# Last projection of a four-layer graph network: centring and scaling of four tiles on GpSimd, VectorE's order laid out anew, transposes one product earlier

## The reference

```python
x_attn = x_attn @ W_proj + b_proj
y = x + x_attn
mu = jnp.mean(y, axis=-1, keepdims=True)
var = jnp.mean(jnp.square(y - mu), axis=-1, keepdims=True)
return (y - mu) * jax.lax.rsqrt(var + LN_EPS) * gamma + beta
...
x = x + _L3_gnn_ref(...) + _L3_mix_ref(xn[None], ...)[0]
x = x + _L3_ffn_ref(_layernorm(x, axis=-1)[None], L3_ffn_Wg, L3_ffn_W1, L3_ffn_W2)[0]
```

## Time and profile before

| | |
|---|---|
| median of three runs | 2966.78 us (2961.51 to 2971.74) |
| span of the profiled execution | 2958.9 us |
| median less span | 7.9 us |
| TensorE busy | 2721.0 us, 92% |
| VectorE busy | 1415.1 us, 48% |
| ScalarE busy | 1128.2 us, 38% |
| GpSimd busy | 704.2 us, 24% |
| this stage's first and last product on TensorE | 2734.86, to 2771.97 |
| its last transposes | 2780.71 to 2782.19 |

### The profile page before, as it was taken

How to read it: one execution, slowest core, us unless ns; L and a number is a source line. 1 busy time by engine, 2 the same in 40 slices (tenths; PEclk the granted TensorE clock), 3 DMA queues, 4 the chain that set the end, 5 groups by cost and what they waited for, 6 DMA issues and landing times.

```text
span 2958.9 us, 48747 instructions
## 1 busy us (share of the span) xinstructions
PE 2721.0 (92%) x20003; PEld 2472.4 (84%) x20003; DVE 1415.1 (48%) x3609; ACT 1128.2 (38%) x2106; POOL 704.2 (24%) x260
## 2 busy tenths in 40 slices
PE   8999999997769999998999899989997999999797
PEld 8999999994339878998888899989676888795697
DVE  8777565573122135568733632231665564105632
ACT  6633265551003213329431342232654243445231
POOL 0134311110002412220334143324112341103121
PEclk9999999998799999999999999999999999999899
DMA  2022221017981112220121122212001121100121
GB/s 69 12 76 79 86 71 38 30 46 280 414 333 57 59 33 55 65 83 26 44 69 50 60 65 76 76 54 76 17 9 52 54 81 49 36 22 23 33 65 59
DMA packets 163790, 220.37 MB, mean 74 GB/s; under 512 B 21521, under 2 KB 142795, under 8 KB 163570
## 3 DMA queue, kind: packets, MB, share of 16 engines
q1 hardware_dynamic: 163570, 217.26, 22.1%
HBM read 215.31 MB, written 1.92 MB: 73 GB/s over the span
## 4 chain that ended last, share of the span: by engine, by line
PE 58%; DVE 7%; ACT 3%; DMA 2%; issue 2%; POOL 1%; SPq 0%; DVEq 0%; ACTq 0%; POOLq 0%
PE ps L58 41%; PE ps L1968 3%; DMA expert_regions<-in_L_ffn_w 2%; PE ps L1882 2%; PE ps L2134 1%; PE ps L2272 1%; PE ps L2155 1%; PE ps L690 1%; PE ps L609 1%; PE ps L599 1%; ACT buf L1079 1%; PE ps L698 1%; DVE buf L2011 1%; DVE buf L2020 1%; PE ps L2916 1%
## 5 line engine op out<-in xcount | busy, mean ns | idle before, releaser
L58 PE MATMUL ps<-weights_r,buf_r 128*125 128x256 f32 (+3 forms) x4050 | 538.6, 284 | 5.7 <-POOL weights_r L276 1.9
L276 POOL TENSOR_TENSOR weights_r<-weights,weights_r 128x1536 fp32r<-128x1536 f32 (+1 forms) x79 | 273.6, 3463 | 1042.8 <-ACT weights_r L269 1029.4
L58 PEld LDWEIGHTS ps<-weights_r,buf_r 128*125 128x125 f32 (+1 forms) x4050 | 508.1, 186 | 9.0 <-issue 4.2
L276 POOL TENSOR_TENSOR weights_r<-weights,head_weights_r 128x1536 fp32r<-128x1536 f32 (+1 forms) x77 | 270.3, 3510 | 1021.7 <-ACT head_weights_r L269 1013.2
L58 PE MATMUL ps<-xT_r,weights_r 128*128 128x376 f32 (+1 forms) x2100 | 345.4, 310 | 0.0
L58 PEld LDWEIGHTS ps<-xT_r,weights_r 128*128 128x128 f32 x2100 | 313.4, 188 | 4.8 <-issue 2.8
L58 PE MATMUL ps<-head_weights_r,buf_r 128*125 128x256 f32 (+2 forms) x2310 | 316.1, 283 | 0.0
L58 PEld LDWEIGHTS ps<-head_weights_r,buf_r 128*125 128x125 f32 x2310 | 293.3, 187 | 0.0
L58 PE MATMUL ps<-weights_r,xT_r 128*125 128x256 f32 x1680 | 233.3, 282 | 8.0 <-issue 4.8
L269 ACT ACTIVATE head_weights_r<-weights 128x1536 fp32r<-128x1536 f32 (+1 forms) x77 | 112.8, 1465 | 306.1 <-PE ps L58 193.1
L58 PEld LDWEIGHTS ps<-weights_r,xT_r 128*125 128x125 f32 x1680 | 212.8, 186 | 10.3 <-issue 5.4
(11 more groups left out here) (368 smaller groups left out, 4310.2 us busy)
## 6 DMA issues: line engine op xcount, KB each, us to landing
expert_regions<-in_L_ffn_w SPq DMA_DIRECT2D x64, 576.0 KB, 15.3
expert_regions<-in_L_ffn_w SPq DMA_DIRECT2D x48, 768.0 KB, 20.5
weights<-in_L_mix_fc_w SPq DMA_DIRECT2D x24, 768.0 KB, 4.5
weights<-in_L_gnn_W SPq DMA_DIRECT2D x18, 768.0 KB, 4.6
weights<-in_L_ffn_W SPq DMA_DIRECT2D x12, 768.0 KB, 4.7
weights<-in_L_mix_w_mapT SPq DMA_DIRECT2D x9, 768.0 KB, 4.8
weights<-in_L_gnn_W_out SPq DMA_DIRECT2D x9, 768.0 KB, 4.5
weights<-in_L_mix_kqv_wT SPq DMA_DIRECT2D x9, 768.0 KB, 4.6
```

The lines of the kernel that those rows point to most:

```text
L58: mm = net.nc.tensor.matmul(ps, net.r(stationary(s, k)), net.r(moving(m, k)), start=(n == 0 and k == 0), stop=(stop and n == 2 and k == kc ...
L276: self.nc.gpsimd.tensor_tensor(self.r(load.dst), load.dst, self.r(load.high), ALU.subtract).then_inc(self.low_made, 1)
```

## The change

`scaled` of tiles 0 to 3 leaves VectorE. GpSimd does it in two steps, `centred` (y - mean, a tensor_scalar with the column of means) and `scaled` (times the row of gamma, a tensor_tensor), each 125 x 768, behind `mean`; `sum` waits for the second. Tile 4 keeps its one-instruction `scaled` on VectorE, now ahead of `inverse`. VectorE's other steps are laid out anew: inverse, sum, stats, mean2 of tile t-1 come behind the second moments of tile t; inverse2 and shift of tile t-1 behind the mean of tile t. ScalarE follows: high(t-2) and root2(t-1), then root(t), then norm(t-1), and at the end high(3) comes ahead of root2(4). TensorE's turn(t-2) comes behind product(0, t). GpSimd waits for gamma and does its eight steps between the two places where it splits weights.

```diff
-        self.order = {e: [] for e in ("pe", "act", "dve")}
-        pe, act, dve = (self.order[e] for e in ("pe", "act", "dve"))
+        self.order = {e: [] for e in ("pe", "act", "dve", "pool")}
+        pe, act, dve, pool = (self.order[e] for e in ("pe", "act", "dve", "pool"))
         for t in range(NT):
             for n in range(len(units)):
                 pe.append(("product", NT * n + t))
-                if n == 1 and t > 1:
+                if n == 0 and t > 1:
                     pe += [("turn", t - 2, g) for g in range(2)]
                 dve += [("add", NT * n + t), ("moments", NT * n + t)]
-                if n == 0 and t > 0:
-                    dve += [("inverse2", t - 1), ("shift", t - 1)]
-                    act += [("norm", t - 1)] + [("high", t - 2, g) for g in range(2) if t > 1]
+                if n == 1 and t > 0:
+                    dve += [("inverse", t - 1), ("sum", t - 1), ("stats", t - 1, 0), ("stats", t - 1, 1), ("mean2", t - 1)]
+                    act += [("high", t - 2, g) for g in range(2) if t > 1] + [("root2", t - 1)]
             dve.append(("mean", t))
+            act.append(("root", t))
+            if t < NT - 1:
+                pool += [("centred", t), ("scaled", t)]
+            if t > 0:
+                dve += [("inverse2", t - 1), ("shift", t - 1)]
+                act.append(("norm", t - 1))
             if t > 1:
                 dve += [("low", t - 2, g) for g in range(2)]
-            dve += [("inverse", t), ("scaled", t), ("sum", t), ("stats", t, 0), ("stats", t, 1), ("mean2", t)]
-            act += [("root", t), ("root2", t)]
-        dve += [("low", NT - 2, g) for g in range(2)] + [("inverse2", NT - 1), ("shift", NT - 1)] + [("low", NT - 1, g) for g in range(2)]
-        act += [("high", NT - 2, g) for g in range(2)] + [("norm", NT - 1)] + [("high", NT - 1, g) for g in range(2)]
-        pe += [("turn", t, g) for t in (NT - 2, NT - 1) for g in range(2)]
+        last = NT - 1
+        dve += [("scaled", last), ("inverse", last), ("sum", last), ("stats", last, 0), ("stats", last, 1), ("mean2", last)]
+        dve += [("low", last - 1, g) for g in range(2)] + [("inverse2", last), ("shift", last)] + [("low", last, g) for g in range(2)]
+        act += [("high", last - 1, g) for g in range(2)] + [("root2", last), ("norm", last)] + [("high", last, g) for g in range(2)]
+        pe += [("turn", t, g) for t in (last - 1, last) for g in range(2)]
...
             elif kind == "scaled":
+                dve.wait_ge(done.sem, done.issued)
                 dve.wait_ge(self.gamma.sem, self.gamma.value)
...
             elif kind == "sum":
                 dve.wait_ge(done.sem, done.issued)
+                if t < NT - 1:
+                    dve.wait_ge(self.net.pool.sem, self.at["pool"]["scaled", t])
...
     def gpsimd(self, pool):
         self.net.split_low(self.weights[-1].unit, self.weights[-1].segment)
+        pool.wait_ge(self.gamma.sem, self.gamma.value)
+        nc, done = self.nc, self.net.pool
+        for kind, t in self.order["pool"]:
+            if kind == "centred":
+                self.wait(pool, "dve", "mean", t)
+                ins = nc.gpsimd.tensor_scalar(self.y[:, t], self.y[:, t], self.net.mv[:, t, 0:1], None, ALU.subtract)
+            else:
+                pool.wait_ge(done.sem, done.issued)
+                ins = nc.gpsimd.tensor_tensor(self.y[:, t], self.y[:, t], self.gamma.dst[:TP, 0], ALU.mult)
+            ins.then_inc(done.sem, done.one())
         for load in self.weights[1:]:
             self.net.split_low(load.unit + 2, load.segment)
```

More of the change, by code:

```diff
@@ L1122, in __init__ @@
                 pe.append(("product", NT * n + t))
-                if n == 1 and t > 1:
+                if n == 0 and t > 1:
                     pe += [("turn", t - 2, g) for g in range(2)]
                 dve += [("add", NT * n + t), ("moments", NT * n + t)]
-                if n == 0 and t > 0:
-                    dve += [("inverse2", t - 1), ("shift", t - 1)]
-                    act += [("norm", t - 1)] + [("high", t - 2, g) for g in range(2) if t > 1]
+                if n == 1 and t > 0:
+                    dve += [("inverse", t - 1), ("sum", t - 1), ("stats", t - 1, 0), ("stats", t - 1, 1), ("mean2", t - 1)]
+                    act += [("high", t - 2, g) for g in range(2) if t > 1] + [("root2", t - 1)]
             dve.append(("mean", t))
+            act.append(("root", t))
[4 more added lines that the diff above has]
+                act.append(("norm", t - 1))
             if t > 1:
                 dve += [("low", t - 2, g) for g in range(2)]
-            dve += [("inverse", t), ("scaled", t), ("sum", t), ("stats", t, 0), ("stats", t, 1), ("mean2", t)]
-            act += [("root", t), ("root2", t)]
-        dve += [("low", NT - 2, g) for g in range(2)] + [("inverse2", NT - 1), ("shift", NT - 1)] + [("low", NT - 1, g) for g in range(2)]
-        act += [("high", NT - 2, g) for g in range(2)] + [("norm", NT - 1)] + [("high", NT - 1, g) for g in range(2)]
-        pe += [("turn", t, g) for t in (NT - 2, NT - 1) for g in range(2)]
-        bases = dict(pe=net.pe.planned, act=net.act.planned, dve=net.dve.planned)
+        last = NT - 1
[3 more added lines that the diff above has]
+        pe += [("turn", t, g) for t in (last - 1, last) for g in range(2)]
+        bases = dict(pe=net.pe.planned, act=net.act.planned, dve=net.dve.planned, pool=net.pool.planned)
         self.at = {e: {q: bases[e] + i + 1 for i, q in enumerate(seq)} for e, seq in self.order.items()}
```

## The result

The changed kernel takes 2969.07 us (median of 20 runs, 2965.41 to 2973.63), beside 2964.50 us for the kernel before in as many runs of the same series. The ratio is 1.0017, its 95% interval 1.0010 to 1.0023: some 5 us slower (3 to 7). In a later series, with some of the experiments, the same kernel gave 1.0029 (1.0019 to 1.0038). The forecast was 5.95 us slower, 2972.7 us.

A forecast was written before the change was run, and what follows sets the result against it. TensorE was taken to bound the stage up to the last product, VectorE's chain the tail; mean(4) +6.26 us and tail -0.31 gave +5.95, so 2966.78 + 5.95 = 2972.7 us, range 2964 to 2980.

The forecast's parts named there:

- What bounds: In the stage, TensorE sets the time up to the last product, 6.96 us a tile; a shorter VectorE list buys nothing.
- The loop: Turn, product 1, VectorE's block, third add, mean, shift, norm, next turn: 8.72 us against TensorE's 6.96, so TensorE waits.
- GpSimd's pair: centred 2.13 us, gap 0.26, scaled 1.82; hidden in the loop with 0.96 us to spare, costing 0.30 on tile 0.
- Rival 1: GpSimd late: centred takes 2.94 us, tile 0's sum comes 0.81 later; +6.8 us, 2973.5 us; chance 10%.
- Rival 3: GpSimd's centred, just ahead of VectorE's shift, holds it by the shared port: 2.17 us three times, 2979.2 us; chance 6%.
- The clock in the loop: TensorE about 80% busy in the loop keeps full clock, so nothing charged; 3 us of spread to either side carried.
- The tail: From mean(4) to turn(4), 7.37 us against 7.68 before: net -0.31, as high(3) no longer stands behind root2(4).
- The sum: Waits and tail added up: mean(4) +6.26 us, turn(4) at 2786.66, +5.95, everything behind it unchanged.

The follow-up runs named there:

- e5_both_back: Changed kernel with turn behind product 1 again and scaled back on VectorE, leaving VectorE's and ScalarE's new order; ratio 1.0004 to the kernel before.
- e9_first_on_dve: Changed kernel with scaled of tile 0 alone back on VectorE, behind mean(0), tiles 1 to 3 staying on GpSimd; ratio 1.0016 to the kernel before.
- e3_scaled_on_dve: Changed kernel with scaled of every tile back on VectorE, behind low(t-2), new orders and the turn's earlier place kept; ratio 1.0005 to the kernel before.
- e7_loop_longer: Changed kernel with nothing on GpSimd and scaled on VectorE between inverse and sum, inside the loop; ratio 1.0029 to the kernel before.
- e1_turn_back: Changed kernel with turn(t-2) behind product 1 of tile t again, VectorE's new order and GpSimd's steps kept; ratio 1.0012 to the kernel before.

## Why the prediction was right, point by point

- *What bounds.* Right. TensorE set the time up to the last product: e5_both_back, with VectorE's order changed and its load full, ends as the kernel before. That a shorter VectorE list brings nothing is shown inside the loop only: three scaled on GpSimd or on VectorE give the same places (e9_first_on_dve, e3_scaled_on_dve). In the old order no run took them off VectorE.
- *The loop.* Right in kind, and nearly in size: 8.72 us forecast, 8.84 and 8.80 measured in the two profiles, 8.80 with the clock undisturbed. The third add was to stand 6.08 behind the turn's start and stands 6.26 and 6.21 behind it in the two tiles at full clock (2769.25 - 2762.99, 2778.04 - 2771.83). e7_loop_longer shows that it is this loop: one instruction moved into it and 1.0 us more each time. turn(0) was forecast at 9.50 from mean(0) and came at 9.49.
- *GpSimd's pair.* 2.13 + 0.26 + 1.82 = 4.21 forecast, 2.21 + 0.08 + 1.85 = 4.14 measured, sum(0) at 4.67 behind mean(0) against 4.60. Rival 1 (2.94 for centred) did not occur. That the pair is hidden in the loop, with 0.96 to spare, held: tile 2's ended at 2765.75, 1.26 ahead of its sum (2767.01). What I did not see is that 4.60 and the 3.16 from sum to mean are a loop of their own, 7.7 long, ready to bind as soon as the first is cut; I had both terms on the page and used them for tile 0 only. It cost the forecast nothing and the expectation of e1_turn_back 3 us.
- *The port.* Rival 3 did not occur: shift took 212 to 215 ns in all five tiles, as before. In three of them GpSimd's centred started beside it (2761.57 and 2761.61, 0.17 before shift's end), and took 2.20 us, against 2.21 in tile 0 with no shift beside it: neither held the other. But shift was first each time, by 0.04 us, and rival 3 priced the other order, which these two instructions have in no run. For GpSimd first, the evidence is five of the sixty rows of 125x1, those from 2075.3 to 2079.2: the other fifty-five ran with GpSimd idle. The Trainium skill's sentence that tensor_scalar can take both ports (SBUF — State Buffer, "Who interferes with whom") showed in none of these 125x1 rows; whether it would with centred first stays open.
- *The clock in the loop.* Wrong: "I charge nothing for the loop". It fell once, behind the first wait, and cost 1.49 us (10.33 - 8.84). The row that I leaned on the earlier trace rows is of a stretch whose waits are shorter (1.39 to 1.56 us within it, 1.75 just ahead of it) than the first one here (1.90). A mean share over 10 us didn't carry over to a single longer gap. The spread of 3 us that I carried for the clock, reckoned for the tail, took it in.
- *The tail.* 7.37 forecast, 7.28 measured (7.68 before): high(3) ahead of root2(4) is worth its 0.7, less the two steps that came in.
- *The sum.* turn(4) was to come 5.95 later and came 7.68 later: 1.49 of the clock, 0.33 in the length of the loop, less 0.09 in the tail. Behind it 0.6 came back in the router's part (43.02 + 177.55 to the end against 35.34 + 178.14 before), and the whole, 7.1 from mean(0) to the end, reads as 1.0017 and 1.0029 in the two series. The median of 2969.07 lies 3.6 under 2972.7; 2.3 of that is that the kernel before came out at 2964.50 in this series and not at 2966.78. That the ratio of 1.0017 (5 us, 3 to 7) comes so near to +5.95 is partly luck: the clock's 1.49 us were left out, and by the places (7.1) or the later series (1.0029, 8.6 us) the loss is above the forecast, not below it.

## What to carry to other kernels

When orders are written out by hand across engines, look for the loops: follow each wait back until it reaches the same step one tile earlier, add up the durations, and compare with the bounding engine's time per tile. Work moved between engines outside the longest of these loops buys nothing: three scaled on either engine gave the same places here. A step moved one product earlier, harmless alone, closed one of 8.8 us with an order that was harmless alone too, over an engine that needs 7.0. And the gain lay where the bounding engine stood idle: in the tail, where reordering two engines' lists brought 3 us with nothing moved to GpSimd.

## What the runs showed of the hardware

- TensorE's clock fell from 2.4 to 1.2 GHz for 3.4 us behind one wait of 1.9 us in otherwise dense work (changed kernel, twice) and at the end of one of 2.61 (e7_loop_longer), and did not behind one of 1.56 in the same place (e3_scaled_on_dve, e9_first_on_dve); the next two waits, of 1.56 to 2.64 in the same kernels, brought none. 0.34 us of waiting so cost 1.9 us at turn(4) and 3.0 by the end.
- The stretch at 1.2 GHz over the stage's first product, behind 4.8 us of idle, stands at the same place in all eleven profiles: from 10.5 to 7.1 us ahead of mean(0), to 0.2 us.
- Between executions mean(0) comes at anything from 2743.2 to 2754.4 us, though all the work ahead of the stage is the same. From there on the places repeat to hundredths. A change inside one stage of some 50 us is read far more sharply from such a common mark than from the whole time.
- On GpSimd a tensor_scalar with a column, one step, 125 x 768, takes 2.20 to 2.21 us, and the dependent tensor_tensor starts 0.08 behind it; behind the two-step form of before it started 0.26 later.
